# An attention and feed-forward kernel: the products with V of two units joined, and the side jobs regrouped

## The reference

```
def _attention(x, W_q, W_k, W_v, W_o):
    q = split(x @ W_q.T)
    k = split(x @ W_k.T)
    v = split(x @ W_v.T)
    attn = softmax(scale * einsum('bnqd,bnkd->bnqk', q, k), axis=-1)
    o = einsum('bnqk,bnkd->bnqd', attn, v)
    ...
    return o @ W_o.T
def _swiglu(x, gate_w, hidden_w, out_w, out_b):
    return silu(x @ gate_w.T) * (x @ hidden_w.T) @ out_w.T + out_b

x = x + a_alpha * _attention(_ada_rmsnorm(x, t, ...), W_q, W_k, W_v, W_o)
x = x + f_alpha * _swiglu(_ada_rmsnorm(x, t, ...), gate_w, hidden_w, out_w, out_b)
out = layernorm(x) * weight + bias, a tanh of the condition added, again * weight + bias
```

## Time and profile before

| | us |
|---|---|
| median of 3 runs | 765.31 |
| the runs | 764.29 to 766.41 |
| the profiled execution | 765.27 |
| its span | 763.5 |

### The profile page before, as it was taken

How to read it: one execution, slowest core, us unless ns; L and a number is a source line. 1 busy time by engine, 2 the same in 40 slices (tenths; PEclk the granted TensorE clock), 3 DMA queues, 4 the chain that set the end, 5 groups by cost and what they waited for, 6 DMA issues and landing times.

```text
span 763.5 us, 17526 instructions
## 1 busy us (share of the span) xinstructions
PE 715.5 (94%) x6660; PEld 489.1 (64%) x6660; DVE 536.7 (70%) x797; ACT 471.2 (62%) x860; POOL 392.2 (51%) x493
## 2 busy tenths in 40 slices
PE   6698889899999999999999999999999999999995
PEld 5433334467676667676767677766676667678894
DVE  4777777777677866777686767767777776436765
ACT  4357677786666766675667756666665665743431
POOL 4354142543376634855367543856267454872533
PEclk9879999999999999999999999999999999999998
DMA  7577566365434644265444554255343640232210
GB/s 225 167 209 241 174 217 215 104 213 169 148 102 140 188 134 167 65 211 147 137 157 138 176 149 153 60 196 153 126 148 120 187 108 5 79 103 60 56 43 29
DMA packets 63132, 107.18 MB, mean 140 GB/s; under 512 B 10464, under 2 KB 18072, under 8 KB 63048
## 3 DMA queue, kind: packets, MB, share of 16 engines
q1 hardware_dynamic: 61892, 104.79, 43.6%
q10 hardware_dynamic: 1028, 1.07, 0.5%
q0 software_dynamic: 128, 0.20, 0.1%
HBM read 57.50 MB, written 37.52 MB: 124 GB/s over the span
## 4 chain that ended last, share of the span: by engine, by line
PE 73%; DVE 10%; issue 7%; ACT 6%; DMA 3%; POOL 1%; ACTq 0%; POOLq 0%; DVEq 0%
PE ps_x L1391 17%; PE ps_j L1278 12%; PE ps_o L1364 12%; PE ps_s L1351 10%; PE ps_j L1404 10%; PE ps_m L1336 7%; DVE mx L1096 3%; ACT prob L892 3%; PE ps_o L1404 2%; DVE fx L1062 2%; DVE gate_t L1136 2%; DMA prob<-in_wk 1%; PE ps_m L1391 1%; PE ps_s L1391 1%; DVE act_y L1143 1%
## 5 line engine op out<-in xcount | busy, mean ns | idle before, releaser
L1096 DVE TENSOR_REDUCE mx<-ps_m 128x2 f32<-128x1024 f32 x222 | 271.7, 1224 | 118.5 <-PE ps_m L1336 118.0
L892 ACT ACTIVATE prob<-ps_s 128x1024 f32<-128x1024 f32 x256 | 262.0, 1024 | 75.4 <-PE ps_s L1351 72.8
L1364 PE MATMUL ps_o<-prob,v 128*32 128x512 f32 x1024 | 137.2, 608 | 0.2 <-ACT o_raw L900 0.2
L1351 PE MATMUL ps_s<-qs,ks 64*128 64x512 f32 x512 | 119.8, 464 | 18.1 <-ACT prob L892 14.1
L1351 PEld LDWEIGHTS ps_s<-qs,ks 64*128 64x128 f32 x512 | 48.4, 185 | 135.7 <-issue 76.8
L1391 PE MATMUL ps_x<-n,gh_hi 64*128 64x256 f32 x872 | 97.7, 284 | 1.7 <-DVE act_y L1143 1.6
L607 POOL TENSOR_TENSOR a_lo<-act_y,a_hi 128x256 fp32r<-128x256 f32 x100 | 73.6, 737 | 46.6 <-ACT a_hi L923 46.4
L1336 PE MATMUL ps_m<-ks,qs 64*128 64x512 f32 x444 | 91.7, 409 | 6.1 <-DVE mx L1096 4.2
L1391 PE MATMUL ps_x<-n_x,gh_hi 64*128 64x256 f32 x872 | 94.3, 276 | 0.0
L632 POOL TENSOR_TENSOR xr<-xr,sc 128x512 f32<-128x512 f32 x41 | 53.2, 1298 | 59.5 <-DVE sc L1108 40.5
L1391 PEld LDWEIGHTS ps_x<-n,gh_hi 64*128 64x128 f32 x872 | 74.2, 184 | 13.7 <-DVE act_y L1143 10.2
(11 more groups left out here) (182 smaller groups left out, 1441.1 us busy)
## 6 DMA issues: line engine op xcount, KB each, us to landing
qs<-stack_scratch SPq DMA_DIRECT2D x30, 512.0 KB, 4.6
ks<-stack_scratch SPq DMA_DIRECT2D x30, 512.0 KB, 6.8
stack_scratch<-qk_hi SPq DMA_DIRECT2D x56, 256.0 KB, 3.1
out_scratch<-o_raw SPq DMA_DIRECT2D x32, 256.0 KB, 3.5
n_x<-n SPq DMA_DIRECT2D x32, 256.0 KB, 3.7
stack_scratch<-qk_lo SPq DMA_DIRECT2D x28, 256.0 KB, 3.4
on_lo<-out_scratch SPq DMA_DIRECT2D x16, 256.0 KB
...
```

The source lines that it names most:

```text
L892: act.activation(prob[:, n % 2, 2 * h:2 * h + 2, :], ps_s[:], ACT.Exp, scale=SCALE).then_inc(p_r, 1)
L1096: dve.tensor_reduce(mx[:, group % 2, :, h, qt], max_pair(mp)[:], AX.X, ALU.max).then_inc(mx_red, 1)
L1351: mm = pe.matmul(ps_s[:, s, :], ks[r:r + 64, g, j, kb * P:(kb + 1) * P], qs[r:r + 64, g, j, :], start=True, stop=True)
L1364: mm = pe.matmul(ps_o[32 * i:32 * i + 32, :], v[:, g, kb, i, :], prob[:, n % 2, i, :], start=(kb == 0), stop=(kb == TT - 1), skip_group_ch ...
```

## The change

**Pairs.** `attend` is no longer issued in every middle unit: an even unit n issues `attend(n - 2)` and `attend(n - 1)` one behind the other at its end, and an odd unit issues none (the last unit, 127, issues `attend(126)`). `prob` has three buffers for that.

**V.** V is stored 17 wide (16 columns and one of ones) in place of 32, and each product reads a window of 32 columns that runs into the next head; the extra output rows aren't read. `gate_t` and `junk` are dropped for the space: tanh writes `act_y` and the gate works there in place, so it is now tanh, on ScalarE, that waits for `a_low(e - 2)`, and no longer the second gate operation on VectorE.

**Jobs.** Chunks move one unit earlier, to u = 1, 5, 9 and 13, and go to `ps_o`. `MIDDLE` replaces the table in middle units: MT, then the chunk, then Q (u = 1, 5) or FT (u = 9, 13) in one row; V, WO, V and TR at u = 3, 7, 11 and 15; TR, K, WO and K at u = 0, 4, 8 and 12; nothing at u = 2, 6, 10 and 14. `TURN` sets the jobs of units 28, 29, 30 and 34. A Q, FT or TR that ends an odd unit is a late job: it is emptied in the next unit, on ScalarE behind exps 0 and on VectorE behind the first reduction.

**Maxima** run seven ahead from unit 30; units 28 and 29 have three each. `RING` is 5 in place of 6. Some DMAs of SP and copies of GpSimd move by a unit.

```diff
+MIDDLE = {0: (("TR", 1, 1),), 1: (("MT", 1, 0), ("Q", 0, 1)), 3: (("V", 0, 1),), 4: (("K", 0, 1),),
+          5: (("MT", 2, 0), ("Q", 1, 1)), 7: (("WO", 0, -1),), 8: (("WO", 1, -1),), 9: (("MT", 3, 0), ("FT", 0, -1)),
+          11: (("V", 1, 1),), 12: (("K", 1, 1),), 13: (("MT", 0, 1), ("FT", 1, -1)), 15: (("TR", 0, 2),)}
...
-CHUNK_AT = GH_AT + CH + LAG
-RING = 6
+CHUNK_AT = GH_AT + CH + 1
+RING = 5
...
+def late_job(n):
+
+    if GH_AT <= n < NU and n % 2 and order_at(n) and order_at(n)[-1][0] in ("Q", "FT", "TR"):
+        return order_at(n)[-1]
+    return None
...
-        v = sb("v", [P, NG, TT, HG, 32])
+        v = sb("v", [P, NG * TT * HG * VW + 32 - VW])
...
-        prob = sb("prob", [P, 2, HG, T])
+        prob = sb("prob", [P, 3, HG, T])
...
+            if n < GH_AT + 2:
+                first = 2 * (GH_AT + LEAD) + 3 * (n - GH_AT)
+                return range(first, first + 3)
+            return range(2 * (n + LEAD + 1), min(2 * (n + LEAD + 1) + 2, 2 * NU))
...
                 act.wait_ge(gh_full, e + 1)
-                if e >= 1:
-                    act.wait_ge(y_r, e)
-                act.activation(gate_t[:], g_part(e), ACT.Tanh, scale=0.5).then_inc(t_r, 1)
+                if 2 <= e < TAIL + 2:
+                    act.wait_ge(a_lo_r, e - 1)
+                elif e >= TAIL + 2:
+                    act.wait_ge(a_tail_r, e - 1 - TAIL)
+                act.activation(act_y[:, e % 2, :], g_part(e), ACT.Tanh, scale=0.5).then_inc(t_r, 1)
...
                 if kb == 0:
-                    pe.wait_ge(v_c, group + 1)
+                    pe.wait_ge(v_c, group + (1 if g == NG - 1 else 2))
                     if group > 0:
                         pe.wait_ge(o_r, group)
+                    if chunk_at(n + 1) is not None:
+                        pe.wait_ge(sc_r, SC_NO["F", chunk_at(n + 1)])
                 for i in range(HG):
-                    mm = pe.matmul(ps_o[32 * i:32 * i + 32, :], v[:, g, kb, i, :], prob[:, n % 2, i, :],
+                    at = ((g * TT + kb) * HG + i) * VW
+                    mm = pe.matmul(ps_o[32 * i:32 * i + 32, :], v[:, at:at + 32], prob[:, n % 3, i, :],
                                    start=(kb == 0), stop=(kb == TT - 1), skip_group_check=True)
...
             def middle_unit(n):
+                maxima = maxima_at(n)
                 scores(n, 0)
-                if n + LEAD < NU:
-                    max_scores(2 * (n + LEAD))
+                for mp in maxima[:1]:
+                    max_scores(mp)
                 gate_hidden(n - GH_AT)
                 scores(n, 1)
-                if n + LEAD < NU:
-                    max_scores(2 * (n + LEAD) + 1)
-                if chunk_at(n) is not None:
-                    project_chunk(chunk_at(n))
-                job(n)
-                attend(n - 1)
+                for mp in maxima[1:]:
+                    max_scores(mp)
+                for what in order_at(n):
+                    if what[0] == "F":
+                        project_chunk(what[1])
+                    else:
+                        job(what)
+                if n % 2 == 0 and n > GH_AT:
+                    attend(n - 2)
+                if n % 2 == 0 or n == NU - 1:
+                    attend(n - 1)
```

More of the change, by code:

```diff
@@ L22 @@
 DT = 64
+VW = DH + 1
 HID = 4 * D
@@ L76, in chunk_at, with order_at @@
     return c if n >= CHUNK_AT and (n - CHUNK_AT) % CH == 0 and c < CHUNKS else None
+def order_at(n):
+    jobs = jobs_at(n)
+    chunk = [("F", chunk_at(n))] if chunk_at(n) is not None else []
+    return [job for job in jobs if job[0] == "MT"] + chunk + [job for job in jobs if job[0] != "MT"]
+def late_job(n):
+    if GH_AT <= n < NU and n % 2 and order_at(n) and order_at(n)[-1][0] in ("Q", "FT", "TR"):
+        return order_at(n)[-1]
+    return None
 SC = sorted([(CHUNK_AT + CH * c, 0, ("F", c)) for c in range(CHUNKS)]
             + [(GH_AT + LAG + JC * (hf + 1), 0, ("H", hf)) for hf in range(CHUNKS * CH // JC, 2 * B)]
-            + [(n, 1, job_at(n)) for n in range(LAST) if job_at(n) and job_at(n)[0] == "WO"])
+            + [(n, 1, job) for job, n in JOB_UNIT.items() if job[0] == "WO"])
 SC_NO = {what: no + 1 for no, (_, _, what) in enumerate(SC)}
@@ L491, in unit @@
                     stack_write(b + 1, 1)
-                if at(7, 1):
+                if at(7, 1) and n < GH_AT:
                     stack_read(b + 1, 0)
@@ L495, in unit @@
                     max_rows(b, 2)
+                if at(6, 1) and n >= GH_AT:
+                    stack_read(b + 1, 0)
+                if at(7, 1) and n >= GH_AT:
+                    stack_write(b + 1, 2)
                 if at(8, 1):
@@ L501, in unit @@
                     o_read(b, 0)
-                if at(10, -1):
+                if at(10 if n < GH_AT or n >= NU else 11, -1) and JOB_UNIT["FT", 0, b - 1] + 3 > n:
                     swap_halves(b - 1, 0)
@@ L510, in unit @@
                     rec_read(b, 0)
-                if at(11, 1):
+                if at(11, 1) and n < GH_AT:
                     stack_write(b + 1, 2)
@@ L525, in unit @@
                     max_rows(b + 1, 0)
-                if at(15, 1):
+                if at(14 if b > 1 else 15, 1):
                     stack_read(b + 1, 2)
@@ L766, in unit @@
                     add_bias(b - 1, 1)
-                if at(14, 1):
+                if at(15 if b == 1 else 14, 1):
                     for g in range(NG - 1):
@@ L787, in _, with square @@
             squared = [0]
-            def square(x, out, made):
+            def square(x, out, made, unread):
                 squared[0] += 1
@@ L800, in square1 @@
             def square1(b, t):
+                if t == 0 and b > 1:
+                    act.wait_ge(n_lo_r, 2 * b)
                 if b == 0 and t == 0:
@@ L807, in square1 @@
                         act.wait_ge(rstd1_r, b - 1)
-                square(xa[:, t, :], ss1[:, b % 2, t:t + 1], sq1)
+                square(xa[:, t, :], ss1[:, b % 2, t:t + 1], sq1, act_y[:, 0] if b < 2 else junk)
             def square2(b, h, t):
@@ L998, in unit @@
                     square2(b - 1, 0, 1)
-                if job_at(n) and GH_AT <= n < NU:
-                    evac(job_at(n), n)
+                for job in jobs_at(n) if GH_AT <= n < NU else []:
+                    if job != late_job(n):
+                        evac(job, n)
                 if u == 0 and 0 < n <= NU:
@@ L1231, in unit @@
                     statistics(b - 3, 1)
-                if chunk_at(n) is not None:
-                    scale(("F", chunk_at(n)))
-                if job_at(n) and n < NU:
-                    evac(job_at(n), n)
+                for what in order_at(n) if n < NU else []:
+                    if what[0] == "F":
+                        scale(what)
+                    elif what != late_job(n):
+                        evac(what, n)
                 if at(3 if b == 1 else 2, -1):
@@ L1504, in _, with job @@
             last = [("TR", 0, 1)]
-            def job(n):
-                if job_at(n) and mt_bank(n) is ps_j:
+            def job(what):
+                if what:
                     job_evacuated(last[0])
-                    run(job_at(n), n)
-                    last[0] = job_at(n)
-                elif job_at(n):
-                    pe.wait_ge(s_r, n - GH_AT + 1)
-                    run(job_at(n), n)
+                    run(what)
+                    last[0] = what
             def early_unit(n):
-                maxima = early_maxima(n)
+                maxima = maxima_at(n)
                 scores(n, 0)
@@ L1552, in tail_units @@
                         project_tail(d)
-                job(n + 1)
+                job(job_at(n + 1))
             for n in range(GH_AT):
```

109 lines of the change are left out of this document (62 added, 47 removed).

## The result

The changed kernel takes 773.56 us (median, 773.07 to 773.88) against 765.86 for the kernel before beside it (764.29 to 767.34): ratio 1.010, 95% interval 1.0078 to 1.0123. It is slower by 1.0%, where the forecast was 761.6, and it lies above the range of 750 to 772.

The account below looks back on a forecast made before the run. TensorE, busy 94%, was taken to bound the kernel. Batches 3 to 5 -2.8, batch 6 -1.2, batch 2 +0.2, batch 7 -3.4, the turn +3.5: -3.7, so 765.27 becomes 761.6; 8-in-10 range 750 to 772.

Parts of the forecast that it names:

- DMAs that move: Transfers moved on SP and GpSimd: priced at nothing, K being wanted some 20 us later, the swap having 0.7 to spare.
- the turn: Units 28 to 31: 17.0 of matmuls and 6.0 of waits, 23.1 against 19.58, a loss of 3.5 us.
- third maxima: Units 28 and 29: each third maxima waits for the reduction before it in the one `ps_m`, 1.5 us twice.
- A pair: Two products with V in one row on TensorE: 1.88 us (1.78 to 1.92), eight per batch saving 1.0.
- rival 2: Bare weight loads at a pair's added passes: 5 to 11 us over 50 pairs, 767 to 773; chance 0.12.
- the loop over `ps_x`: From a unit's second maxima to the next gate matmuls at least 2.50 us pass, so short odd units must wait.
- the 1.0 for u = 0: From u = 15 to 0, only 1.48 us of work stands behind the second maxima, so TensorE waits 1.0.
- 82.1 of work and 4.3 of waits: TensorE in each of batches 3 to 5: matmuls 2.3 less, waits 4.3 against 3.0, together 86.4, 0.9 less.
- Rival 1: The forecast waits don't come: they stay at 2 per batch, the turn costs 1.5, 748 us; chance 0.20.
- Batch 7: The last batch, with few jobs, without unit 127: 70.1 us against 73.4, a gain of 3.4.
- Rival 3: GpSimd's `a_low` holds tanh ahead of exps 1 when a DMA chain is long: 12.6 us, 774; chance 0.13.
- joined jobs: Two Q and two FT directly behind a chunk each save 0.22 us of entry and exit: 0.9 per batch.

Follow-up runs that it names:

- experiment 9: Changed kernel with two staging buffers for rounded Q and K, half of out_w's remainder left out and the other half used twice: 767.04 us, ratio to before 1.0038.
- experiment 1: Changed kernel with SP, from unit 28 on, issuing the write of Q's half at u = 3 ahead of the reciprocals' write and read: 768.19 us, ratio 1.0054.
- experiment 4: Changed kernel with Q's writes ahead of the reciprocals (unit 27; u = 3 from unit 28) and third maxima in units 26, 27 instead of 28, 29: 763.85 us.
- Experiment 11: The kernel of experiment 9 with the third maxima moved from units 28 and 29 to 26 and 27: 760.92 us, ratio to before 0.9955.
- experiment 7: The kernel of experiment 4 with K in unit 29, MT in 30, Q's write at u = 2, and half of the pairs undone: 758.44 us, ratio 0.9927.
- experiments 3: Changed kernel with Q's writes ahead of the reciprocals, in unit 27 and at u = 3 from unit 28 on: 767.58 us, ratio to before 1.0043.

## Why the prediction was wrong

**The step that failed** is the paragraph "DMAs that move". It priced the moved transfers at nothing, because K is *wanted* some 20 us after it is written. That follows a transfer to the reader of its destination. The wait came from the other end: who may overwrite its *source*. The change put K one unit behind Q at the turn, where it stood two behind before. In the batches it put K three units behind Q instead of two, but the write of Q stayed at u = 3 and K moved up to u = 4; the one unit that was left was eaten by SP's order and, in batch 4, by a DMA of 6.5 us. (The write of Q's second half did move up, by four units from u = 11 to u = 7, and no rounding of K at u = 12 waited for it.) It cost 6.1 in batch 2 and 1.3 in batch 4 (experiment 9, with the slow clock behind it). In the turn it cost little while the third maxima waited as well: 26.84 became 26.30 with two buffers, and 27.17 in experiment 1, which leaves the turn as it was, so 0.5 is within what executions differ by. Without the third maxima it cost 1.9 (experiment 4 against 11, 21.85 to 20.00; the two also differ in SP's order).

**The turn was under-sized.** I had 23.1 and it took 26.84. The third maxima were named, at 1.5 for each of two units. Removing them took 6.3 out (26.30 to 20.00, experiments 9 and 11) and put 1.0 into unit 27. In unit 28 of experiment 9, 2.29 pass from the second maxima's start to the job (148.71 to 151.00) where two maxima leave 0.33, so one costs 2.0 instead of 1.5. The larger part is the clock behind them: in experiment 9 the job of unit 28 takes 1.3 more than at full clock, and the gate matmuls of unit 30 take 2.7 instead of 1.4. That term I didn't have at all: the windows of before that I read the earlier trace rows show 1.00 throughout.

**What held.** Batches 3 and 5 at 86.30 and 86.28 (forecast 86.4). A pair takes 1.85 (forecast 1.88), within 1.78 to 1.92, so rival 2 falls. The weight loads of the second product are issued beneath running matmuls of the pair. The timeline of TensorE at u = 14 to 0 shows the last of these loads (row PEld) and the pair, and then the loop over `ps_x` that the prediction counted:

```profile
345.31 0.13 PEld L1420 LDWEIGHTS ps_o<-prob,v 128*32 128x32 f32 x4 [0.30 <-issue]
...
344.42 1.92 PE L1420 MATMUL ps_o<-prob,v 128*32 128x512 f32 x16
346.27 0.50 PE L1404 MATMUL ps_s<-qs,ks 64*128 64x512 f32 x2
...
347.35 0.39 PE L1444 MATMUL ps_x<-n,gh_hi 64*128 64x256 f32 x2 [0.29 <-DVE act_y L1192]
...
350.53 0.50 PE L1404 MATMUL ps_s<-qs,ks 64*128 64x512 f32 x2 [0.43 <-ACT prob L940]
...
351.62 0.39 PE L1444 MATMUL ps_x<-n,gh_hi 64*128 64x256 f32 x2 [0.28 <-DVE act_y L1192]
```

From the maxima to the gate there are 0.7 to 0.8 in u = 15 and 0, instead of 0.23, as forecast in kind; a part of the 1.0 for u = 0 shows as a wait of its first scores (0.43) instead. The total of a batch, 82.1 of work and 4.3 of waits, was right within 0.1 here; of its single terms only the pair and the loop in u = 15 and 0 are read above, so the others may be off and cancel. Rival 1 (a batch at 84) falls with that. For the early units and the tail I expected nothing. The tail, from unit 127 on, took 0.7 more; it is 89.2 to 90.4 in the nine traces with the change's pairs and 88.5 to 89.1 in the three with the old order, so a small loss there may be real. No run was made for it.

**Smaller misses.** Batch 6 took 85.77 instead of 85.1. Batch 7 took 71.95 instead of 70.1: in u = 0, 4 and 12 I had 4.0 to 4.4, but each follows a short odd unit, so the loop makes them 5.0 (4.9 for u = 12). (Some sums of the prediction are 0.1 off by rounding: the units of batch 7 add up to 70.2 and the terms of the turn to 23.0. Nothing hangs on it.) Undoing pairs there gave 0.9 (experiment 7), which fits. Batch 2 without the missed wait is 87.15 instead of 86.7: unit 36 takes 6.5 instead of 6.1, since its gate matmuls on `n_x` start 0.3 late (the step to them is 0.39 instead of 0.12): the swap of FT(1,0) had moved to unit 35.

**Rival 3** was right as a mechanism and is not the cause. In the changed kernel ScalarE was held by K's rounding first. In experiments 3 and 4, where that wait was gone but the reciprocals stood behind the write of Q, tanh waited 2.1 and 2.4 for `a_lo` and unit 37 lost 0.6 to 0.9.

**What the change is worth by itself.** Experiment 11, with the third maxima moved, gives 760.9, beside 761.6 of the forecast. That agreement is luck in part: the turn is 3.1 shorter than forecast (20.00 for 23.1, with 1.0 moved to unit 27), and batches 2, 6 and 7 are 3.0 longer. And the four pairs that were undone have little share in it; the other four weren't undone. A pair takes 0.15 less than two single products, but a pair makes an odd unit short, and what it saves goes into the loop of 2.50, which doesn't get shorter. The gain of a regular batch comes, as far as the runs show, from the other parts; which of these, joined jobs or MT ahead of the chunk, wasn't tried alone.
